# A vision tower in one launch: setup split by need, and the second item's tokens computed during the first reload

## What is computed

```python
h = _L0_tok_ref(x, L0_tok_W)          # patches of 16, stride 8, rfft along time, linear map to 64
h = h + _L0_attn_ref(_layernorm(h), qkv, bias_table)   # 8 heads of 8, softmax, relative bias of period 7
h = h + _L0_ffn_ref(_layernorm(h), ...)  # 64 -> 128, two routed layers (one expert per 256 tokens), -> 64
h = h + _L1_attn_ref(_layernorm(h), ...) # 8 heads of 8, softmax, no bias
h = h + _L1_ffn_ref(_layernorm(h), ...)  # top-2 gate of 8 experts, gelu, 64 -> 128 -> 64
```

## Time and profile before

| | |
|---|---|
| median of the runs | 4351.33 us (4348.1 to 4358.9) |
| the profiled execution: time, span | 4357.37 us, 4355.6 us |
| its mean granted PE clock | 0.975 of full speed |
| busy: PE, DVE, ACT, GpSimd | 3922.3, 2902.0, 2728.0, 858.6 us |
| DMA queue of SP | 152.36 MB, 19.8% of 16 engines' span |

### The profile page before, as it was taken

How to read it: one execution, slowest core, us unless ns; L and a number is a source line. 1 busy time by engine, 2 the same in 40 slices (tenths; PEclk the granted TensorE clock), 3 DMA queues, 4 the chain that set the end, 5 groups by cost and what they waited for, 6 DMA issues and landing times.

```text
span 4355.6 us, 61579 instructions
## 1 busy us (share of the span) xinstructions
PE 3922.3 (90%) x21509; PEld 1300.5 (30%) x21509; DVE 2902.0 (67%) x4956; ACT 2728.0 (63%) x4896; POOL 858.6 (20%) x1263
## 2 busy tenths in 40 slices
PE   2478899999999999999999999999999999999796
PEld 1122232333233232323333332333323233332222
DVE  2356585767768576766867676776767677676561
ACT  0155576766767676666767666676767667676464
POOL 2112221213122121312212131221213122121211
PEclk9599999999999999999999999999999999999898
DMA  2221321131222022122212212221221222121100
GB/s 51 39 45 25 57 38 23 31 57 30 40 47 39 21 36 49 30 40 47 40 25 39 42 30 40 47 40 27 39 40 30 40 47 40 30 32 23 30 1 6
DMA packets 115606, 156.30 MB, mean 36 GB/s; under 512 B 21391, under 2 KB 63119, under 8 KB 115261
## 3 DMA queue, kind: packets, MB, share of 16 engines
q1 hardware_dynamic: 115297, 152.36, 19.8%
HBM read 120.01 MB, written 29.36 MB: 34 GB/s over the span
## 4 chain that ended last, share of the span: by engine, by line
PE 65%; ACT 10%; DVE 8%; issue 8%; DMA 4%; POOL 4%; SPq 1%; POOLq 0%; ACTq 0%; DVEq 0%
PE acc L847 16%; PE st L833 16%; PE nat L813 15%; DVE tile_max L1234 5%; PE side L782 3%; PE side L679 3%; DMA k_rows<-k_scratch 2%; ACT hidden L1004 2%; ACT prob L1031 2%; PE side L656 2%; PE side L768 2%; PE side L736 1%; ACT hidden L949 1%; DVE ln_s L1139 1%; POOL centred L1317 1%
## 5 line engine op out<-in xcount | busy, mean ns | idle before, releaser
L1234 DVE TENSOR_REDUCE tile_max<-nat 128x1 f32<-128x512 f32 x4096 | 2599.1, 684 | 1242.1 <-PE nat L813 1221.6
L1031 ACT ACTIVATE prob<-st 128x512 f32<-128x512 f32 x4096 | 2298.2, 596 | 1429.5 <-PE st L833 1376.1
L833 PE MATMUL st<-q_rows,k_rows 99*128 99x512 bf16 x4096 | 1573.0, 385 | 66.8 <-ACT prob L1031 57.7
L813 PE MATMUL nat<-k_rows,q_rows 96*128 96x512 bf16 x4096 | 1450.7, 386 | 138.9 <-DMA k_rows<-k_scratch 91.3
L847 PE MATMUL acc<-prob,v_padded 128*32 128x512 f32 x8192 | 1098.0, 608 | 1.0 <-ACT prob L1031 1.0
L833 PEld LDWEIGHTS st<-q_rows,k_rows 99*128 99x128 bf16 x4096 | 398.2, 97 | 1313.7 <-ACT prob L1031 1034.2
L813 PEld LDWEIGHTS nat<-k_rows,q_rows 96*128 96x128 bf16 x4096 | 401.9, 98 | 679.5 <-DVE tile_max L1234 345.8
L1387 POOL TENSOR_SCALAR max_parts<-neg_max 128x16 bf16<-128x16 f32 x128 | 26.3, 206 | 1757.2 <-DVE neg_max L1241 1312.6
L847 PEld LDWEIGHTS acc<-prob,v_padded 128*32 128x32 f32 x8192 | 161.5, 108 | 339.5 <-issue 277.6
L1314 POOL TENSOR_SCALAR ln_s<-ln_s 128x8 f32<-128x8 f32 x64 | 13.0, 203 | 1050.6 <-DVE ln_s L1139 1050.6
L782 PE MATMUL side<-hidden,w 128*64 128x512 f32 x512 | 136.5, 616 | 0.0
(11 more groups left out here) (127 smaller groups left out, 2081.2 us busy)
## 6 DMA issues: line engine op xcount, KB each, us to landing
q_rows<-q_scratch SPq DMA_DIRECT2D x288, 128.0 KB
k_rows<-k_scratch SPq DMA_DIRECT2D x96, 384.0 KB
x_rows<-in_x SPq DMA_DIRECT2D x64, 512.0 KB, 6.7
q_scratch<-hidden SPq DMA_DIRECT2D x32, 384.0 KB
k_scratch<-hidden SPq DMA_DIRECT2D x96, 128.0 KB
group_weights<-in_routed SPq DMA_DIRECT2D x64, 129.0 KB, 2.1
q_rows<-max_rows SPq DMA_DIRECT2D x512, 3.0 KB
out_h<-out_rows SPq DMA_DIRECT2D x16, 256.0 KB, 2.1
```

Of the source, the lines that this page charges most:

```text
L813: eng.matmul(NAT[place % len(NAT)][:, :], QA[u][0:K_NAT, h, c:c + P], KA[u][0:K_NAT, h, kh * 512:kh * 512 + 512], start=True, stop=True)\
L833: eng.matmul(ST[n % 2][:, :], KA[u][0:K_ALL, h, t * P:t * P + P], QA[u][0:K_ALL, h, half * 512:half * 512 + 512], start=True, stop=True)\
L1031: eng.activation(prob[:, n % TILES, :], ST[n % 2][:, :], ACT.Exp).then_inc(exp_done, 1)
L1234: eng.tensor_reduce(mx[:, q % 2, j // 8, j % 8 // 2, j % 2:j % 2 + 1], NAT[place % len(NAT)][:, :], AX.X, ALU.max).then_inc(nat_free, 1)
```

## The change

Setup: the loads that the first stages need are counted on the old semaphore (19 DMAs, behind nine of DFT weights and image), 18 others on a semaphore of their own (`s_rest`), and 43 more (projection weights, `b_1`, `b_2`, routes) are issued after the first reload and counted there too; every engine waits for `s_rest` at tile 8 (`LATE`) of "first". The bias parts are made earlier on DVE, in other places of SBUF; the one-hot rows of item 0's operands are issued right after them, those of item 1's after the first reload, each with its own semaphore, for which PE waits at the first natural tile of the item. The second half of item 0's image goes to a place of its own, loaded at the start.

Stages: item 1's two image loads, TOKA, TOKB, TOKC, LN1 and LN2 move from tiles 0 to 30 of "first" into "serial", around item 0's SCR and RL; its TR, QK, QV, VC, SCR are put at tiles 2 to 20 instead of 38 to 60, and its reload at tiles 26 to 48, with SP waiting for the tile's `st` before each DMA.

```diff
@@ -207,14 +207,13 @@
...
-    start = [("TOKA", 0), ("LX", 0, 1), ("TOKB", 0), ("TOKC", 0), ("LN1", 0, "0"),
-             ("LN2", 0, "0"), ("TR", 0, "0"), ("QK", 0, 0), ("QV", 0, 0), ("SCR", 0, 0),
-             ("VC", 0, 0), ("RL", 0, 0), ("HO0", 0)]
+    start = [("TOKA", 0), ("TOKB", 0), ("TOKC", 0), ("LN1", 0, "0"), ("LN2", 0, "0"), ("TR", 0, "0"),
+             ("QK", 0, 0), ("QV", 0, 0), ("LX", 1, 0), ("TOKA", 1), ("SCR", 0, 0), ("VC", 0, 0), ("LX", 1, 1),
+             ("RL", 0, 0), ("HO0", 0), ("TOKB", 1), ("TOKC", 1), ("LN1", 1, "0"), ("LN2", 1, "0")]
     first = {n: [] for n in range(ATTN)}
-    for n, *stages in ((0, ("LX", 1, 0)), (8, ("TOKA", 1), ("LX", 1, 1)), (16, ("TOKB", 1)),
-                       (20, ("TOKC", 1)), (24, ("LN1", 1, "0")), (30, ("LN2", 1, "0")),
-                       (38, ("TR", 1, "0")), (44, ("QK", 1, 0), ("WCL", 0)), (50, ("QV", 1, 0)),
-                       (54, ("SCR", 1, 0), ("VC", 1, 0)), (62, ("RL", 1, 0)), (80, ("WCA", 0))):
+    for n, *stages in ((2, ("TR", 1, "0")), (5, ("QK", 1, 0)), (9, ("QV", 1, 0)),
+                       (13, ("VC", 1, 0)), (14, ("SCR", 1, 0)), (26, ("RL", 1, 0)), (56, ("WCL", 0)),
+                       (80, ("WCA", 0))):
         for k, part in enumerate(side_parts(stages)):
@@ -472,17 +479,15 @@
...
                 for hh in range(2):
-                    eng.dma_start(xt[64 * hh:64 * hh + 64, :, :],
+                    eng.dma_start((x_first if (b, half) == (0, 1) else xt)[64 * hh:64 * hh + 64, :, :],
                                   item.rearrange("c (m h j) v -> c m h (j v)", h=2, j=4)
@@ -495,53 +500,62 @@
...
             load_x(0, 0)
+            load_x(0, 1)
+            twice = (slice(0, 64), slice(64, P))
             load(CT[:, 0:P], const[:, 0:P])
...
             load(scl[:, :], qk_scale)
-            twice = (slice(0, 64), slice(64, P))
             for half in twice:
-                load(WI[half, :], wi[0:64])
-                load(WG[half, :], wg[0:64])
-                load(W1[half, :, :], w1[0:64])
-                for a in (0, 1):
-                    load(WQK[a][half, :], qk_w[a, 0:64])
-                    load(WV[a][half, :], v_w[a, 0:64])
-                    for c in range(HEADS):
-                        for g in range(2):
-                            row, head = half.start + HD * (2 * c + g), HD * (HEADS * g + c)
-                            load(WP[a][row:row + HD, :], pw[a, head:head + HD])
-            load(WO[:, :], wo)
-            load(bob[:, :], bo.unsqueeze(0).to_broadcast([P, 64]))
-            load(WS[:, :, :], shared)
-            load(W2[:, :, :], w2)
-            load(bi[:, :], wi[64].unsqueeze(1))
-            load(bg[:, :], wg[64:65].to_broadcast([P, E]))
-            for e in range(E):
-                load(b1[:, e:e + 1], w1[64, e].unsqueeze(1))
+                load(WQK[0][half, :], qk_w[0, 0:64])
+                load(WV[0][half, :], v_w[0, 0:64])
             for a in (0, 1):
                 load(bqk[a][:, :], qk_w[a, 64].unsqueeze(1))
-                load(bv[a][:, :], v_w[a, 64:65].to_broadcast([P, 64]))
-                load(bp[a][:, :], pw[a, 64:65].to_broadcast([P, 64]))
-            load(routes[:, :], route.unsqueeze(0))
-            N_SET_DMA[0] = n_dma[0]
-            eng.wait_ge(s_dve, SET_DVE)
+            load(bv[0][:, :], v_w[0, 64:65].to_broadcast([P, 64]))
+            load(bp[0][:, :], pw[0, 64:65].to_broadcast([P, 64]))
+            load(W2[:, :, :], w2, s_rest)
+            for half in twice:
+                load(WI[half, :], wi[0:64], s_rest)
+                load(WG[half, :], wg[0:64], s_rest)
+                load(W1[half, :, :], w1[0:64], s_rest)
+                load(WQK[1][half, :], qk_w[1, 0:64], s_rest)
+                load(WV[1][half, :], v_w[1, 0:64], s_rest)
+            load(WO[:, :], wo, s_rest)
+            load(bob[:, :], bo.unsqueeze(0).to_broadcast([P, 64]), s_rest)
+            load(WS[:, :, :], shared, s_rest)
+            load(bi[:, :], wi[64].unsqueeze(1), s_rest)
+            load(bg[:, :], wg[64:65].to_broadcast([P, E]), s_rest)
+            load(bv[1][:, :], v_w[1, 64:65].to_broadcast([P, 64]), s_rest)
+            load(bp[1][:, :], pw[1, 64:65].to_broadcast([P, 64]), s_rest)
+            def onehot_rows(a):
+                for i in range(PARTS):
+                    row = PROD + WINDOW * i
+                    load(QA[a][row:row + WINDOW, :, :],
+                         hot[0:WINDOW, :].unsqueeze(1).to_broadcast([WINDOW, H, N_TOK]), s_rows[a])
+                    load(KA[a][row:row + WINDOW, :, :],
+                         bias_parts[:, i, :].unsqueeze(1).to_broadcast([WINDOW, H, N_TOK]), s_rows[a])
+            def late_loads():
+                for half in twice:
+                    load(B2[half.start + E:half.start + 2 * E, :], b2[0:E], s_rest)
+                    for a in (0, 1):
+                        for c in range(HEADS):
+                            for g in range(2):
+                                row, head = half.start + HD * (2 * c + g), HD * (HEADS * g + c)
+                                load(WP[a][row:row + HD, :], pw[a, head:head + HD], s_rest)
+                for e in range(E):
+                    load(b1[:, e:e + 1], w1[64, e].unsqueeze(1), s_rest)
+                load(routes[:, :], route.unsqueeze(0), s_rest)
+            eng.wait_ge(s_dve, SET_BIAS)
             eng.wait_ge(s_pool, SET_POOL)
-            for half in twice:
-                load(B2[half.start + E:half.start + 2 * E, :], b2[0:E])
-            hot = h0c[0:2 * WINDOW, :, :].rearrange("p j c -> p (j c)").bitcast(BF16)
-            for a in (1, 0):
-                for s in range(PARTS):
-                    row = PROD + WINDOW * s
-                    load(QA[a][row:row + WINDOW, :, :],
-                         hot[0:WINDOW, :].unsqueeze(1).to_broadcast([WINDOW, H, N_TOK]))
-                    load(KA[a][row:row + WINDOW, :, :],
-                         PT[0:WINDOW, s, :].unsqueeze(1).to_broadcast([WINDOW, H, N_TOK]))
-            N_SET_DMA.append(n_dma[0])
-            eng.wait_ge(s_dma, n_dma[0])
+            onehot_rows(1)
@@ -603,6 +619,9 @@
...
                         side_stage(stage, found[0, k])
+                        if stage[0:2] == ("RL", 0) and stage[3] and n0 == 0:
+                            onehot_rows(0)
+                            late_loads()
                     return
@@ -613,7 +632,7 @@
...
                     for k, stage in enumerate(side[n]):
-                        side_stage(stage, found[n, k], n0 + n if kind == "pair" and 0 < it < B - 2 else 0)
+                        side_stage(stage, found[n, k], n0 + n if kind == "first" or kind == "pair" and 0 < it < B - 2 else 0)
@@ -633,13 +652,11 @@
...
-            eng.wait_ge(s_dma, N_SET_DMA[0])
+            eng.wait_ge(s_dma, N_SET[s_dma])
             for a in range(2):
...
                 mm.then_inc(s_pe, 1)
-            eng.wait_ge(s_dve, SET_DVE)
-            eng.wait_ge(s_pool, SET_POOL)
-            eng.wait_ge(s_dma, N_SET_DMA[1])
+            eng.wait_ge(s_dve, SET_WF)
@@ -674,7 +691,7 @@
...
                     bk = side_bank(n, 0)
-                    xv = xt[:, :, :].rearrange("p m (j v) -> p m j v", j=4)
+                    xv = (x_first if half and b == 0 else xt)[:, :, :].rearrange("p m (j v) -> p m j v", j=4)
                     for j in range(4):
@@ -806,6 +823,8 @@
...
                 if q % SUPERS == 0 and j == 0:
+                    if a == 0 and b < 2:
+                        eng.wait_ge(s_rows[u], 2 * PARTS * 16)
                     eng.wait_ge(qk_in[u], at(DMA_QK * (loads_before(a, b) + 1)))
@@ -856,11 +875,15 @@
...
                 if kind == "first":
+                    eng.wait_ge(s_dve, SET_DVE)
+                    eng.wait_ge(s_pool, SET_POOL)
                     for m in range(SUPER + LEAD):
...
                 for n in range(n_tiles(kind)):
+                    if kind == "first" and n == LATE:
+                        eng.wait_ge(s_rest, N_SET[s_rest])
                     for k, stage in enumerate(side[n]):
@@ -1068,9 +1092,18 @@
...
             step(ins)
-            eng.tensor_copy(h0c[0:2 * WINDOW, :, :].rearrange("p j c -> p (j c)").bitcast(BF16),
-                            prob[0:2 * WINDOW, 0:2, :].rearrange("p a c -> p (a c)"))
-            step(eng.tensor_copy(ident_b[:, :], ident))
+            eng.wait_ge(s_dma, N_SET[s_dma])
+            step(eng.tensor_copy(hot, prob[0:2 * WINDOW, 0:2, :].rearrange("p a c -> p (a c)")))
+            eng.wait_ge(s_pe, 4)
+            for a in range(2):
+                ins = eng.tensor_copy(bias_f[:, a * 512:a * 512 + 512], NAT[a][0:WINDOW, :])
+            step(ins)
+            step(eng.tensor_copy(bias_parts[:, 0, :], bias_f))
+            step(eng.tensor_tensor(bias_f, bias_f, bias_parts[:, 0, :], ALU.subtract))
+            step(eng.tensor_copy(bias_parts[:, 1, :], bias_f))
+            step(eng.tensor_tensor(bias_parts[:, 2, :], bias_f, bias_parts[:, 1, :], ALU.subtract))
```

(52 more changed lines are left out.)

1 line of the change is left out of this document (removed).

## The result

| | before | forecast | changed |
|---|---|---|---|
| median of the runs | 4352.83 us | 4245 us | 4244.7 us (4238.9 to 4250.3, four runs) |
| profiled span | 4355.6 us | 4249.4 us | 4237.5 us |
| first patch matmul of item 0 | 90.27 | 23.6 | 24.55 |
| first DMA of the first reload | 145.44 | 69.3 | 68.99 |
| first natural tile | 174.00 | 103.5 | 96.03 |

What follows compares the result with a forecast made beforehand. The steady part was taken as bound by PE's own work, the idle front by DMA or its issue. Terms -70.5 - 37.4 + 1.2 + 0.5 = -106.2 us took the 4351.3 us median to 4245, range 4232 to 4262.

Steps and rivals of the forecast that it cites:

- First patch matmul: Setup, item 0: PE would wait only for Wf, so it starts at 23.6 us instead of 90.3, -66.7 us.
- Item 0's second half in a place of its own: Before the first reload: its image wait goes, -7.7 us, and the block takes the short duration, -3 us.
- Reload issued: First DMA of the first reload: 68.0 us plus 1.3 for item 1's block A and image issue, 69.3 against 145.44.
- The image in front of the reload: Item 1's image half queued before the first reload: 5.6 us taken from 0 to 5.6, first natural tile at 103.5.
- The fit quoted beside this term: Skill page's DMA cost, about 2 us plus bytes over 436 GB/s: reload about 7.4 us; not used for the range.
- SP behind the reload: One-hot copies and 43 late loads before SP's first maximum rows: +1.2 us at tile 0, from 0 to 10.3.
- Rival (a): SP's queue the new bound: tiles 0 and 8 come 10 us later, rows at tile 64 cost 2; 4256 us, chance 0.12.
- The 28.1 us from the first natural tile to tile 0: Natural tiles before tile 0: 28.1 us as before, bound by DVE's maxima, so tile 0 at 131.6 us.
- The first 128 tiles: From tile 0 to the end of tile 127: 104 us instead of 141.4, -37.4 us, plus 0.5 for maximum rows.
- Maximum rows at tile 64: Rows for tiles 64 on, issued at tile 55 behind item 1's reload: 0 to 2 us of wait, 0.5 taken.
- The rest unchanged: Everything after tile 127: same work in the same order in both kernels, 4012 us carried over.
- Clock (rival d): PE's clock stays low after waits: gain gone after 177 slow tiles, 4399 us with all 256 slow; chance 0.01.

Runs made afterwards that it cites:

- setup alone: Changed setup and own place for item 0's second image half, item 1's stages as in the kernel before: 4275.1 us against 4355.1, ratio 0.9816.
- the old setup: Setup of the kernel before, with the stages as in the changed kernel: 4316.4 us against 4355.1, ratio 0.9906.
- 32 more loads: Changed kernel with 32 more 2 KB loads behind the late ones, into a spare tile: 4246.3 us beside 4247.0 for the changed kernel.
- relatives: Here the kernel before's setup with changed stages (4316.4 us), and the changed kernel with item 1's one-hot copies issued in setup (4253.0 us).
- the spaced reload: Changed kernel with the last four DMAs of item 1's reload at tiles 57 to 60 instead of 42 to 48: 4241.0 us, ratio 0.9741.

## Why the prediction was right, and where it wasn't

- **First patch matmul**, 23.6 forecast, 24.55, 24.03 and 24.58 measured: right. The bias matmuls began at 21.05 instead of 20, behind the end of the DFT matmuls.
- **Item 0's second half in a place of its own**: right, with the short duration: 3.67 us behind 1.36 of idleness, against 6.66 behind 8.96.
- **Reload issued**, 69.3 forecast, 68.99, 68.41 and 69.06 measured: the date is right by two small errors that cancel. The +1.3 us for item 1's block A wasn't paid: without block A the reload left at 68.86 (setup alone), and in the old setup at 145.45 with it and 145.44 without. What made up for it is that the first patch matmul came 0.4 to 1.0 us later than forecast and everything up to the reload with it.
- **The image in front of the reload**: the step that failed. Between 0 and 5.6 us I took 5.6, "because both go through one queue"; eight profiles say 0. The trace before already had the counter-argument, which I didn't use: the reload moved 2.36 MB in 28.56 us where an image half moved 1 MB in 5.6, so it didn't fill all engines that the image uses. This is 5.6 of the 7.5 us by which the first natural tile was early; the rest is a reload shorter by 1.6 than the forecast's 28.6, within its own spread, and issued 0.3 earlier. The fit quoted beside this term from the Trainium skill ("DMA: Bandwidth & Descriptors", section "Anatomy of one DMA") is given there for DMAs that GpSimd issues. This kernel's are issued by SP, so 25.1 to 29.7 us against its 7.4 doesn't test it.
- **SP behind the reload**: I took +1.2 of 0 to 10.3; it was 0, with 2.8 to 4.7 us to spare. The terms were mis-sized in both directions: the one-hot copies left SP at 86.8, not 110, and the first 16 projection pieces then took 17.19 us where 16 had cost 6.7. Rival (a) is real in kind, as 32 more loads showed, and missed its place by these 2.8 to 4.7 us.
- **The 28.1 us from the first natural tile to tile 0**: exact in all three profiles.
- **The first 128 tiles**: 104.5 forecast, 103.5, 101.7 and 105.7 measured: right.
- **Maximum rows at tile 64**: 0 to 2 with 0.5 taken; 1.14 in the first profile, but 4.19 and 3.04 in relatives. The bound was too tight. I let the reload's backlog end at tile 64; that it can end later is the likely reason, but the spaced reload didn't settle it.
- **The rest unchanged**: 4012.1 before; 4009.9, 4009.5 and 4004.5 after: right to within 0.2%. All twelve profiles of kernels with the change or a part of it have 4004.5 to 4010.8 here, below the one profile of the kernel before; whether that is more than spread isn't shown.
- **Clock (rival d)**: the lower level lasted 3 to 9 us of tiles, nowhere near the 177 tiles that would have turned the sign.

The sum of dates is -118.1 us in the first profile, 12 more than forecast: 8.7 at tile 0 (5.6 for the image, 1.9 for the reload's issue and length, 1.2 for SP), 1.0 in the first 128 tiles and 2.2 behind them. Yet the median fell on the forecast. Its agreement to within 1 us is luck. The two profiled executions lie 10 us further apart than the medians, which hides most of the 12, and 4244.7 lies in the gap between the two groups of executions, where the changed kernel has none. The trace holds one execution each, all of the lower group, so what the upper group does differently stays open; its mean granted clock is 0.978, against 0.979 to 0.980 in the lower one.

## What to carry to other kernels

Look at what stands in front of the first dense loop as a chain of its own, with one date for each hand-over: here 118 of 4356 us went although no engine did less work. Before pricing two transfers as a sum because they share a queue, compare their rates: a transfer that moves 83 GB/s where its neighbour moves 187 can leave room beside it. Work that is moved behind a transfer also moves in front of whatever the same queue issues next, and its slack has to be counted there.

## What the runs showed of the hardware that was not expected

A small load cost SP 0.34 us of issue when the DMA queue was nearly empty (32 in 10.86 us) and 1.07 on average while a reload and six SBUF copies drained (16 in 17.19 us). Two image DMAs that cost 1.3 to 1.4 us of issue elsewhere cost 5.25 behind one-hot copies. The reload of 2.36 MB took 25.1 to 27.0 us in the three profiles of the changed kernel and up to 29.7 in its relatives.

The granted clock stayed at 0.50, the 1.2 GHz level, through all 28.2 us of the natural tiles, although PE was busy for 27.36 of them by its modelled ends (one natural tile each 0.59 us, held by DVE's maxima). In the changed kernel's profiles it rose only 3.0 to 9.1 us behind tile 0, where a natural and a transposed block followed each other every 0.43 us.
